# Scores against values and the FFN steps regrouped: the 64-channel products of two batches in one step, S in one step, H, Qf, v and Pf in other steps

## What is computed

```
x = x + cross_attention(layernorm(x), ctx)      8 heads of 64: q from x, k and v from ctx,
                                                softmax over the 257 rows, then Wo and bo
x = x + recurrent(layernorm(x) * ln_g + ln_b)   4 heads of 64, 32 steps in each batch:
        state = (1 - w_t) * state + outer(k_t, v_t);  out_t = r_t . state;  then Wo
        w = sigmoid(xn Wx Ww + bw), r = sigmoid(xn Wr)
x = x + V2(U2(gelu(V1(U1(layernorm(x))) + b1))) + b2
```

## Time and profile before

| | us |
|---|---|
| median of 3 runs | 970.79 |
| lowest, highest | 970.17, 971.96 |
| the profiled execution | 969.11 |
| its span in the trace | 967.1 |
| PE busy in it | 943.9 (98%) |

### The profile page before, as it was taken

One profiled execution on the slowest core, in us unless ns is written; L12 is line 12 of the kernel. 1 busy time (PEld: TensorE's weight loads), 2 busy tenths in 40 slices (PEclk: granted clock), 3 DMA queues, 4 the chain that ended last, 5 costly groups with the idle time before them and its releaser, 6 DMA issues.

```text
span 967.1 us, 23520 instructions
## 1 busy us (share of the span) xinstructions
PE 943.9 (98%) x9012; PEld 783.6 (81%) x9012; DVE 613.0 (63%) x1286; ACT 607.3 (63%) x1487; POOL 373.8 (39%) x484
## 2 busy tenths in 40 slices
PE   9999999999999999999999999999999999999998
PEld 7767888787888878798887878888787888877775
DVE  4765858476685847668485666747567584746461
ACT  3545657667575766767576675757757566674533
POOL 1423534244352524435253352524326252433330
PEclk9999999999999999999999999999999999999999
DMA  8314231322323132132222313122222313222000
GB/s 304 120 51 124 59 105 49 100 81 65 105 78 90 51 101 81 60 110 61 88 69 87 95 60 94 60 87 89 81 80 81 90 49 89 87 73 72 9 12 22
DMA packets 58013, 79.03 MB, mean 82 GB/s; under 512 B 10288, under 2 KB 39856, under 8 KB 57904
## 3 DMA queue, kind: packets, MB, share of 16 engines
q1 hardware_dynamic: 56192, 76.38, 25.9%
q10 hardware_dynamic: 1712, 1.16, 0.4%
HBM read 73.05 MB, written 4.46 MB: 80 GB/s over the span
## 4 chain that ended last, share of the span: by engine, by line
PE 78%; DVE 9%; ACT 7%; issue 3%; POOL 1%; DMA 0%; DVEq 0%; POOLq 0%; ACTq 0%
PE gb L369 16%; PE scores L428 7%; PE acc L459 7%; PE gb L492 6%; PE acc L455 6%; PE scores L432 6%; PE ptp L442 5%; PE acc L460 5%; PE gb L613 3%; PE gb L602 3%; DVE xn L840 3%; ACT probs L685 3%; PE gb L401 3%; DVE probs L853 2%; DVE small L846 2%
## 5 line engine op out<-in xcount | busy, mean ns | idle before, releaser
L1100 POOL TENSOR_TENSOR t_l<-raw_t,t_h 128x516 fp32r<-128x516 f32 x128 | 167.5, 1309 | 193.6 <-PE scores L432 131.0
L685 ACT ACTIVATE probs<-scores,small 128x257 f32<-128x257 f32 x256 | 119.1, 471 | 134.6 <-DVE small L846 134.4
L846 DVE TENSOR_REDUCE small<-scores 128x2 f32<-128x514 f32 x128 | 88.3, 690 | 127.5 <-PE scores L432 127.4
L1109 POOL TENSOR_TENSOR ptm<-probs,head 128x32 f32<-128x32 f32 x128 | 35.1, 274 | 261.9 <-DVE probs L853 261.9
L853 DVE TENSOR_TENSOR probs<-probs,small 128x514 f32<-128x514 f32 x128 | 101.7, 794 | 4.4
L459 PE MATMUL acc<-pt,raw_n 128*128 128x256 f32 x256 | 89.6, 431 | 0.0
L442 PE MATMUL ptp<-ident,probs 128*128 128x128 f32 x512 | 78.7, 276 | 10.5 <-DVE probs L853 9.4
L696 ACT ACTIVATE pt<-ptp 128x512 f32<-128x512 f32 x128 | 77.2, 603 | 13.2 <-PE ptp L442 11.7
L455 PE MATMUL acc<-pt,raw_n 128*64 128x128 f32 x1024 | 82.7, 282 | 2.3 <-ACT pt L696 0.4
L428 PE MATMUL scores<-t_h,qk_h 128*128 128x258 f32 x256 | 83.3, 325 | 0.0
L455 PEld LDWEIGHTS acc<-pt,raw_n 128*64 128x64 f32 x1024 | 55.4, 136 | 31.9 <-issue 21.0
(11 more groups left out here) (178 smaller groups left out, 2768.8 us busy)
## 6 DMA issues: line engine op xcount, KB each, us to landing
raw_t<-in_ctx_t SPq DMA_DIRECT2D x128, 258.0 KB, 3.3
raw_n<-in_ctx_n SPq DMA_DIRECT2D x128, 192.0 KB, 2.4
xb<-in_x SPq DMA_DIRECT2D x16, 256.0 KB, 4.3
vsp<-tail_values SPq DMA_DIRECT2D x256, 2.0 KB
out<-ob SPq DMA_DIRECT2D x16, 256.0 KB, 2.9
xin<-in_x SPq DMA_DIRECT2D x15, 256.0 KB, 2.9
khat<-in_wq ACTq DMA_DIRECT2D x1, 512.0 KB, 4.3
wv<-in_wv SPq DMA_DIRECT2D x1, 512.0 KB, 6.3
```

The source lines that it names most:

```text
L685: go(probs[n % 2][:, r, 0:L], scores[:, r, 0:L], ACT.Exp, bias=nmax[:, r:r + 1], accum_out=rsum[:, r:r + 1]).then_inc(s["exp_ready"], 1)
L846: v_.tensor_reduce(nmax[:], scores[:, :, 0:L], AX.X, ALU.max, negate=True)\
L1100: p_.tensor_tensor(t_l[m % 2][:], raw_t[m % RING][:], t_h[m % 2][:].bitcast(F32), ALU.subtract)\
```

## The change

- `pv(n)` makes the last 64 channels not of its own batch but of those that RESTS lists: steps 0 and 1 their own, steps 3, 5 and 7 those of two batches (2 and 3, 4 and 5, 6 and 7), steps 2, 4 and 6 none. The product of the earlier of two batches goes to columns 128 to 255 of its half of acc.
- The transposed probabilities of batches 2, 4 and 6 are kept in the memory of `xn0` (`pt_late`), so DVE's `xn0` waits for the last `pv` of the group before. `pc_out` on ACT copies 128x256 in steps 2, 4, 6, and in steps 3, 5, 7 has one more copy, of 128x128. `load_n` is issued when the 64-channel product of its buffer is done, so in steps 3, 5 and 7 two of them.
- Sp and Sq become one step S in step 7, which writes two banks in full instead of four by half; DVE's four masked copies of 128x256 become two of 128x512, both in gap 1 of step 7.
- Qf goes from step 0 of the next block to step 7; H0 and H2 from step 7 to step 6; Pf from step 6 to step 4; v from step 6 to step 5. On DVE i2 goes from step 6 to step 5. The emptying of the pipeline (ENDING) follows suit.

The diff, without its unchanged surroundings:

```diff
@@ -37,16 +37,19 @@
 PREP, HERE, POST, FFN, END = 1, 0, -1, -2, -3
-FILL1 = [["Sq", "Qf", "WV"], ["O2"], [], ["Qa0"], ["Qa1"], ["Qb"], [], ["Sp", "H0", "H2"]]
-FILL2 = [["St"], ["Y3", "Y1", "XT"], ["Y2", "XT2", "q0", "q2"], ["z", "q1", "q3", "XT3"], ["k"], ["r"], ["Pf", "v"],
+FILL1 = [["WV"], ["O2"], [], ["Qa0"], ["Qa1"], ["Qb"], ["H0", "H2"], ["S", "Qf"]]
+FILL2 = [["St"], ["Y3", "Y1", "XT"], ["Y2", "XT2", "q0", "q2"], ["z", "q1", "q3", "XT3"], ["k", "Pf"], ["r", "v"], [],
          ["TP"]]
+RESTS = [[0], [1], [], [2, 3], [], [4, 5], [], [6, 7]]
 NEXT, OLD, OLDER = NG - 1, NG - 2, NG - 3
-ENDING = {(NG, 0): [("Sq", OLD), ("WV", NEXT), ("St", OLD)],
-          (NG, 1): [("Y1", NEXT), ("Qf", OLDER), ("O2", OLD), ("Y3", OLDER)], (NG, 2): [("XT2", NEXT), ("Y2", OLD)],
+ENDING = {(NG, 0): [("WV", NEXT), ("St", OLD)],
+          (NG, 1): [("Y1", NEXT), ("O2", OLD), ("Y3", OLDER)], (NG, 2): [("XT2", NEXT), ("Y2", OLD)],
           (NG, 3): [("z", NEXT)], (NG, 4): [("k", NEXT), ("XT3", OLD)], (NG, 5): [("r", NEXT), ("Pf", OLD)],
-          (NG, 6): [("v", NEXT)], (NG, 7): [("Sp", NEXT)], (NG + 1, 0): [("Sq", NEXT), ("St", NEXT)],
+          (NG, 6): [("v", NEXT)], (NG, 7): [("S", NEXT)], (NG + 1, 0): [("St", NEXT)],
           (NG + 1, 1): [("O2", NEXT), ("H0", OLD)], (NG + 1, 2): [("Y2", NEXT), ("H2", OLD), ("Qf", OLD)],
@@ -56,19 +59,19 @@
...
 BUSY = {("XT", 0): 3, ("Qa1", 0): 3, ("Qb", 0): 5, ("WZ", 0): 4,
-        ("Y3", OLDER): 1, ("Y2", OLD): 2, ("v", NEXT): 6, ("Sq", NEXT): 2, ("St", NEXT): 2, ("H0", OLD): 1,
+        ("Y3", OLDER): 1, ("Y2", OLD): 2, ("v", NEXT): 6, ("S", NEXT): 2, ("St", NEXT): 2, ("H0", OLD): 1,
         ("H2", OLD): 3, ("Qf", OLD): 1, ("Pf", NEXT): 2, ("H2", NEXT): 1, ("Qf", NEXT): 1}
...
 TILES.update({n: [n + "e", n + "o"] for n in ("Qa0", "Qa1", "Qb")})
-TILES.update({"Sp": ["S0", "S1"], "Sq": ["S2", "S3"], "St": ["St0", "St1"]})
+TILES.update({"S": ["S0", "S1"], "St": ["St0", "St1"]})
 SHIFT = {"XT": PREP, "TP": HERE}
...
 SHIFT.update({n: PREP for n in ("Qa0", "Qa1", "Qb")})
-SHIFT.update({n: POST for n in "WV Y1 XT2 z k r v Sp".split()})
-SHIFT.update({n: FFN for n in "Sq St O2 Y2 XT3 Pf H0 H2".split()})
-SHIFT.update({n: END for n in ("Qf", "Y3")})
+SHIFT.update({n: POST for n in "WV Y1 XT2 z k r v S".split()})
+SHIFT.update({n: FFN for n in "St O2 Y2 XT3 Pf H0 H2 Qf".split()})
+SHIFT["Y3"] = END
 FIRST, LAST = -1, NG + 1
@@ -118,7 +121,17 @@
-DECAYS = 5
+DECAYS = 6
+def rests(n):
+    return [n - n % G + b for b in RESTS[n % G]]
+def sums(n):
+    return sum(1 + 2 * len(rests(m)) for m in range(n + 1))
@@ -187,6 +200,8 @@
...
+        pt_late = xn0[:].rearrange("p t d -> p (t d)").rearrange("p (t m) -> p t m", t=LT)
         hid = sb("hid", [P, 8, T])
@@ -219,6 +234,9 @@
...
+        def pt_of(n):
+            return pt if n in rests(n) else pt_late
@@ -282,7 +300,10 @@
...
                 if n >= RING:
-                    sp.wait_ge(s["acc_ready"], 3 * (n - RING + 1))
+                    step = n - RING
+                    while n - RING not in rests(step):
+                        step += 1
+                    sp.wait_ge(s["acc_ready"], sums(step))
                 sp.dma_start(raw_n[n % RING][:], ctxn_v[n]).then_inc(ctxn_in[n % RING], 16)
@@ -332,8 +353,9 @@
...
                         load_t(n + RING + 1)
-                    if n + RING < B:
-                        load_n(n + RING)
+                    for m in rests(n):
+                        if m + RING < B:
+                            load_n(m + RING)
                     if b == 5 and i < NG:
@@ -448,16 +470,18 @@
...
                     pe.wait_ge(s["pc_ready"], n)
-                x = raw_n[n % RING]
-                for t in range(LT):
-                    for k in range(2):
-                        last = mm(acc[64 * k:64 * k + 64, 1, 0:P], x[:, t, P:C], pt[:, t, k * P:(k + 1) * P],
-                                  start=t == 0, stop=t == 1)
-                        if t == 1:
-                            last.then_inc(s["acc_ready"], 1)
-                mm(acc[:, 0], x[:, 0, 0:P], pt[:, 0], start=True, stop=False)
-                mm(acc[:, 0], x[:, 1, 0:P], pt[:, 1], start=False, stop=True).then_inc(s["acc_ready"], 1)
+                for m in rests(n):
+                    c0 = P * (n - m)
+                    for t in range(LT):
+                        for k in range(2):
+                            last = mm(acc[64 * k:64 * k + 64, 1, c0:c0 + P], raw_n[m % RING][:, t, P:C],
+                                      pt_of(m)[:, t, k * P:(k + 1) * P], start=t == 0, stop=t == 1)
+                            if t == 1:
+                                last.then_inc(s["acc_ready"], 1)
+                x, p_ = raw_n[n % RING], pt_of(n)
+                mm(acc[:, 0], x[:, 0, 0:P], p_[:, 0], start=True, stop=False)
+                mm(acc[:, 0], x[:, 1, 0:P], p_[:, 1], start=False, stop=True).then_inc(s["acc_ready"], 1)
@@ -539,27 +563,27 @@
...
-            def s_tiles(c, g):
-                even, odd = tile(f"S{2 * c}", g), tile(f"S{2 * c + 1}", g)
+            def s_tiles(g):
+                even, odd = (tile(n, g)[:].rearrange("p a (c k) -> p (a c) k", k=P) for n in ("S0", "S1"))
                 pe.wait_ge(s["hat_ready"], HATS * (g + 1))
...
                 for t in range(2):
-                    t_ = slice(t * P, (t + 1) * P)
-                    for i in range(NB):
-                        keys = i * 2 * T + c * T + t * P
-                        queries = i * 2 * T // NB + (2 * c + t) * 32
-                        for r0, out_ in ((0, even), (64, odd)):
-                            last = mm(out_[32 * i:32 * i + 32, 0, t_],
-                                      rhat[r0:r0 + 64, queries:queries + 32],
-                                      khat[r0:r0 + 64, keys:keys + P], start=True, stop=True)
-                            if (t, i) == (1, NB - 1):
-                                done(f"S{2 * c + r0 // 64}", g, last)
+                    for c in range(2):
+                        for i in range(NB):
+                            keys = i * 2 * T + c * T + t * P
+                            queries = i * 2 * T // NB + (2 * c + t) * 32
+                            for r0, out_ in ((0, even), (64, odd)):
+                                last = mm(out_[32 * i:32 * i + 32, 2 * t + c], rhat[r0:r0 + 64, queries:queries + 32],
+                                          khat[r0:r0 + 64, keys:keys + P], start=True, stop=True)
+                                if (t, c, i) == (1, 1, NB - 1):
+                                    done(f"S{r0 // 64}", g, last)
...
                     out_ = tile(f"St{t}", g)
-                    drained("S3", g)
+                    drained("S1", g)
                     for h in range(4):
@@ -629,7 +653,7 @@
...
             steps["St"] = turn_s
-            steps["Sp"], steps["Sq"] = lambda g: s_tiles(0, g), lambda g: s_tiles(1, g)
+            steps["S"] = s_tiles
             for j in range(2):
@@ -693,17 +717,20 @@
...
                 act.wait_ge(s["pt_ready"], n + 1)
-                go(pt[:], ptp[:], ACT.Copy).then_inc(s["ptev_ready"], 1)
+                go(pt_of(n)[:, :], ptp[:], ACT.Copy).then_inc(s["ptev_ready"], 1)
             def pc_out(n):
-                act.wait_ge(s["acc_ready"], 3 * n + 3)
-                b = n % G
-                go(pc[:, :, b * S:(b + 1) * S],
-                   acc[:].rearrange("p c (h s) -> p (c h) s", h=H)[:, 0:H + H // 2], ACT.Copy)\
+                act.wait_ge(s["acc_ready"], sums(n))
+                b, own = n % G, n in rests(n)
+                if len(rests(n)) > 1:
+                    go(pc[:, H:, (b - 1) * S:b * S], acc[:, 1, P:2 * P].rearrange("p (h s) -> p h s", s=S), ACT.Copy)
+                columns = H + H // 2 if own else H
+                go(pc[:, 0:columns, b * S:(b + 1) * S],
+                   acc[:].rearrange("p c (h s) -> p (c h) s", h=H)[:, 0:columns], ACT.Copy)\
                     .then_inc(s["pc_ready"], 1)
             def step(name, g):
-                if name in ("Y1", "Y2", "Y3", "TP", "Sp", "Sq"):
+                if name in ("Y1", "Y2", "Y3", "TP", "S"):
                     return
@@ -875,6 +902,8 @@
...
                         dve.wait_ge(bank_filled[bank], k)
+                    if g > 1:
+                        dve.wait_ge(s["acc_ready"], sums((g - 1) * G - 1))
                     norm_apply(xin, 0, g, xn0)
@@ -944,10 +973,9 @@
...
                     t = wait_tile(n, g)
-                    c, e = int(n[1]) // 2, int(n[1]) % 2
-                    drain(n, g, v_.copy_predicated(s_q[:, 2 * c + e:2 * c + e + 5:4],
-                                                   mask[:].rearrange("p (o q) -> p o q", o=1).to_broadcast([P, 2, P]),
-                                                   t[:, 0].rearrange("p (t q) -> p t q", t=2)))
+                    drain(n, g, v_.copy_predicated(s_q[:, int(n[1])::2],
```

(26 more changed lines are left out.)

## The result

| | before | after |
|---|---|---|
| median, us | 970.71 (4 runs) | 982.12 (4 runs) |
| lowest to highest | 970.17 to 971.96 | 981.44 to 982.22 |
| span of the profiled execution | 967.1 | 979.6 |

The ratio is 1.0114, 95% interval 1.0097 to 1.0132: slower by 11.4 us, where 10 were forecast (981, range 969 to 988).

The account below looks back on a forecast made before the run. TensorE's program plus its waits was taken as the bound, each step also limited by its chain after the score. Twelve blocks at +0.5 us plus the ends made +10: 979 profiled, median 981, range 969 to 988.

Parts of the forecast that it names:

- The saving on TensorE: TensorE work per block: 0.8 us less, bounds 0.5 and 1.1, if TensorE stays the bound everywhere.
- the one for the pairs: Pairing of 64-channel products: 0.16 us of tiling change and refill dropped three times per block, 0.48.
- the 0.3 for two fewer changes of tiling: Moves of S, Qf and H: two fewer changes of array tiling per block, 0.15 to 0.2 us each.
- Step 2: Loses 0.59 us of TensorE work but stays 6.97; its chain from Y1 through xn1 to the maxima is untouched.
- Steps 3, 4 and 5: Step 3 gets +0.43 us; steps 4 and 5 grow by 0.27 and 1.87, with neither chain binding.
- v's wait for i2: Step 5, v's drain behind i2: taken as 0; would cost 0.6 us with its cover gone.
- Step 0: Loses S of two heads and Qf: -2.38 us; its chain had 4 us to spare.
- Steps 6 and 7: From step 6's last score record, s, batch 8's turn comes at s + 11.0 us, +0.3, 0.9 after TensorE is ready.
- the string: ACT's gapless instructions from batch 7's Exp to batch 8's, with Gelus and table loads: 7.93 us, setting batch 8's turn.
- The ends: Block 0: 0; block 1: +1.3 us; block 2: +2.3; block 15: -0.6; emptying of the pipeline: +0.9.
- the normalisation of batch 8: Rival for step 7: POOL's work lengthens this normalisation, 0.9 us more in each of 13 blocks, 993; chance 0.07.
- the hidden Gelus: Rival for steps 6 and 7: ACT ends early, 0.9 us less in 13 blocks, 969.5, no change; chance 0.08.
- TensorE as the bound: Rival for every step: only the 0.8 us of tilings counts in 14 blocks, -11, near 960; chance 0.07.

Follow-up runs that it names:

- e2_tanh: Changed kernel with Tanh in place of Gelu in H's drain, so ACT loads no table there (computes another function): 969.2 us, 0.9984 of the kernel before.
- e3_xn1: Changed kernel with xn1 moved from gap 0 to gap 1 of DVE's step 2, behind the maxima of the next scores: 971.57 us, 1.0004.
- e1_own: Changed kernel with the pairing alone undone, every step making its own 64-channel products: 978.28 us, 1.0074 of the kernel before.
- f1_best: Kernel before with xn1 in gap 1 and only batches 1 with 2 and 3 with 4 paired, late probabilities in rt: 961.08 us, 0.9901.
- f2_order: Changed kernel with xn1 in gap 1, POOL's high part also in step 7, pairs 1 with 2, 3 with 4, 5 with 6: 959.49 us, 0.9886.
- e7_bxn1: Kernel before with xn1 moved to gap 1 of step 2 alone: 962.51 us, 0.9919.
- e8_own: Changed kernel with xn1 in gap 1, POOL's high parts in steps 6 and 7, and the pairing undone: 970.88 us, 1.0003.
- f4_last: Changed kernel with xn1 in gap 1, POOL's high part also in step 7, pairs 3 with 4 and 5 with 6 only: 959.49 us, 0.9889.

## Why the prediction was right

**The saving on TensorE.** 0.8 us a block was forecast, between 0.5 and 1.1, and a busy time near 933. The centre was too high. The windows of a block hold 56.32 of busy time, against 56.77 (the seven of the earlier trace rows and 8.34 of step 1), 0.45 less; the page has 938.5, not 933. Both understate the saving: matmul records 0.28 long start 0.12 apart, so a record ahead of a wait counts some 0.16 of busy time that otherwise lies under the next one, and the page holds the stretch at half the clock (last section). `e2_tanh`, whose steps 6 and 7 do not wait, gives 0.6: the windows of its block hold 56.16. `e3_xn1`, whose profiled execution kept the full clock, has 935.0 on its page. So it is about 0.6, inside the range. Of the two terms the one for the pairs holds: 0.14 for one by steps 4 and 5 of `e1_own`, for 0.16. What was mis-sized is the 0.3 for two fewer changes of tiling by the moves of S, Qf and H; no more than 0.15 to 0.2 of it is seen. The time did not feel it, because steps 2 and 7 wait in any case. `f1_best` adds that such a saving depends on the neighbours.

**Step 2.** That it gives nothing back: 6.97 became 6.98. By `e1_own` and `e3_xn1` the cause is the chain through xn1, as argued. The sign that was named, 0.8 of wait ahead of the turn, is 0.43 in the trace: part of the wait has moved to XT2, which the prediction did not have, and 0.16 lies under the end of the last record.

**Steps 3, 4 and 5.** 0.43, 0.27 and 1.87 were forecast; 0.43, 0.29 and 1.85 measured. v's wait for i2 cost nothing.

**Step 0.** -2.38 forecast, -2.29 measured. Of the 0.09, 0.06 is in WV's first eight records (524.95 to 525.97, for 519.79 to 520.75), which now follow another tiling.

**Steps 6 and 7.** The turn was to come at s + 11.0, and came at 11.03; the string was to take 7.93, and took 7.95; TensorE was to be ready at s + 10.1, and `e2_tanh` shows it at 10.1. The Exp of batch 8 ended 0.98 before its turn, with the two masked copies (1.36 us together) long done. The idle time ahead of the turn reads 0.63, where 0.9 was named; the overlap of records accounts for 0.16 of the rest. From the load's start to the Gelu's it is 1.29 us, and without the two loads the string is 2.83 shorter, 1.4 for each. What the page of the Trainium skill adds to a table load as drain (ScalarE: Activation LUTs, "What ACT_TABLE_LOAD costs"), some 1.38 us, is not in this kernel either.

**The ends.** Block 1 was +1.3 (measured 51.08 for 49.80), block 2 +2.3 (56.81 for 54.52). Blocks 3 to 14 were forecast at +0.5 each and came to +0.62, 7.4 together instead of 6. The term that was mis-sized is what lies behind block 14: +0.3 was forecast and +1.5 measured (block 15 up to the last turn 0.3 shorter, the rest 1.8 longer). Two things are in it that the forecast did not have. The last S waits 1.3 us for a Gelu's drain, since S's bank is one that H had filled four tiles before:

```profile
916.52 0.66 PE L464 MATMUL ptp<-ident,probs 128*128 128x128 f32 x4
918.52 1.15 PE L578 MATMUL gb<-khat,rhat 64*32 64x128 f32 x64 [1.34 <-ACT hid L794]
```

In the steady blocks, where the score of the next batch stands between, H is drained in time, and in `e2_tanh`, without the table loads, the wait is gone. The other is the clock, below, 1.1 us. The two are more than the 1.2 by which the term was short, so the rest of it came out about 1.2 lower than forecast. The blocks gave 1.4 more than forecast and the end 1.2 more; the profiled execution is 2.4 over the forecast of 979, at 981.4. The mechanism of the blocks was right; that the end term is off by no more than 1.2 is luck, since 2.4 us that it did not have stand against 1.2 that it had too much.

The three rivals: the Gelus were not hidden; TensorE was not the bound throughout; the normalisation of batch 8 took 0.69 us, so it was not lengthened. The chances were added up with two of them exchanged: by the list the hidden Gelus, which mean no change, have 0.08 and TensorE as the bound, which means faster, has 0.07.

## What to carry to other kernels

In a program whose steps each have a dependent chain beside the main engine's work, a cut of work is worth what it leaves above the chain of that step: list for every step the cover and the chain before moving anything, and count a moved instruction's whole train on the other engines (here eight Gelus with two table loads) against the step that it comes to. Then look for the cheap edit first: the order of two instructions on an engine with a third of its time idle was worth 8 us in the kernel before, more than all the regrouping on TensorE. The regrouping paid, by at most 3 us, only once the pairs stood elsewhere and part of the late chains had been moved aside, and a merged phase saves a change of tiling only if its neighbours have another one (`f1_best`). And a total that comes out as expected does not show that its parts did (`f2_order`): compare the steps.

## What the runs showed of the hardware

TensorE's clock fell for a while near the end of the changed kernel. In block 15 step 2 ends in a wait of 1.86 us, as in the kernel before. The windows of TensorE (length, busy, granted clock, DMA) of step 2, the first 3.2 us of step 3, and the rest of it, in the changed kernel:

```profile
885.07:892.48 7.41, 5.00 (x38) 0.99 0.40 127
892.48:895.70 3.22, 3.22 (x16) 0.50 0.01 3
895.70:899.62 3.92, 3.92 (x39) 1.00 0.15 43
```

and of the kernel before, step 2 and the start of step 3, in its profiled execution:

```profile
876.32:883.72 7.40, 5.54 (x46) 1.00 0.34 89
883.72:886.50 2.78, 2.78 (x26) 1.00 0.31 116
```

It went from 2.4 to 1.2 GHz after a step in which TensorE was busy for 5.00 of 7.41 us, and not, in this one execution, after one with 5.54 of 7.40. Step 3 of block 15 took 7.14 us with it and 6.04 in `e3_xn1` (pairing kept, no fall there), so the fall costs about 1.1 us.

It is tempting to put the fall down to the change, and the mean granted clock of the other executions speaks against that. One such fall makes the mean 0.998, as here. Of the 51 executions of the kernel before that ran beside the experiments 24 show 0.997 or 0.998, at a median of 971.2 us, and 27 show 1.000, at 970.0. So the kernel before has such a fall in about half of its executions, at the same price, and its profiled one happened to have none. Of the changed kernel all four show 0.998, and of `e1_own`, with the pairing undone, three of four.

What the kept traces have in common is the wait in front. Up to the last turn of batches, every fall to half the clock follows a turn that waited 1.74 us or more: in block 15 the turn of step 3 (1.86 us, wherever xn1 is not moved), in block 0, and once in block 1, the turn of step 7 (1.74 us, in all kernels that pair 4 with 5 and 6 with 7). Five kernels have neither of these two waits (`e7_bxn1`, `e8_own`, `f1_best`, `f2_order`, `f4_last`), and all their 27 executions show 0.999 or 1.000. Of the 48 executions of the changed kernel and of the seven runs that have one or both, 38 show 0.998 or less. The same kernel with the same wait falls in some executions and not in others, and no run varies such a wait alone, so what decides the single fall stays open.
